# Saving the last states of seven scans on VectorE instead of ScalarE

## The reference

```
delta = softplus(dt @ wdt.T + bdt)
A = -exp(Alog)
dA = exp(delta[..., None] * A)                          # [rows, 1024 channels, 16 states]
dBu = (delta * u)[..., None] * Bm[:, :, None, :]
def step(h, t):
    h = dA_t * h + dBu_t
    return h, einsum('bdn,bn->bd', h, C_t)              # y of one row
```

## Time and profile before

| | |
|---|---|
| median of 3 runs | 7626.0 us (7614.66 to 7628.69) |
| the profiled execution | 7626.0 us, span 7624.1 us |
| TensorE | busy 6846.7 us, 90% |
| VectorE | busy 6908.3 us, 91% |
| ScalarE | busy 6185.3 us, 81% |
| GpSimd | busy 6963.5 us, 91% |
| mean granted TensorE clock | 0.972 |

### The profile page before, as it was taken

How to read it: one execution, slowest core, us unless ns; L and a number is a source line. 1 busy time by engine, 2 the same in 40 slices (tenths; PEclk the granted TensorE clock), 3 DMA queues, 4 the chain that set the end, 5 groups by cost and what they waited for, 6 DMA issues and landing times. The chain is left out here.

```text
span 7624.1 us, 137978 instructions
## 1 busy us (share of the span) xinstructions
PE 6846.7 (90%) x32682; PEld 4032.5 (53%) x32682; DVE 6908.3 (91%) x9409; ACT 6185.3 (81%) x12569; POOL 6963.5 (91%) x3774
## 2 busy tenths in 40 slices
PE   6899989999898989999898999999888999999889
PEld 3455555555555555555555555555555555555455
DVE  2799999999899999999899999999899999999766
ACT  1788888888888888888788888888888888888645
POOL 0899999999899999999999999999999999999678
PEclk8999999999999999999999999999999999999989
DMA  8444445444444553444445544444354444444555
GB/s 257 145 137 131 128 139 150 109 138 139 128 134 127 147 148 107 141 139 137 122 127 149 148 104 144 137 136 133 119 150 140 112 144 135 136 133 130 147 194 171
DMA packets 605613, 1066.05 MB, mean 140 GB/s; under 512 B 113584, under 2 KB 221872, under 8 KB 596336
## 3 DMA queue, kind: packets, MB, share of 16 engines
q1 hardware_dynamic: 602704, 1055.84, 46.9%
q10 hardware_dynamic: 2080, 1.05, 0.0%
HBM read 926.61 MB, written 130.05 MB: 139 GB/s over the span
## 5 line engine op out<-in xcount | busy, mean ns | idle before, releaser
L692 POOL TENSOR_TENSOR dBu<-Bb,du 128x1024 f32<-128x1024 f32 x2048 | 4786.0, 2364 | 80.0 <-DVE hV L1177 45.4
L1177 DVE TENSOR_TENSOR_SCAN scans<-scans,state,dBu 128x512 f32<-128x512 f32 x2304 | 2907.6, 1283 | 453.0 <-ACT scans L808 374.6
L808 ACT ACTIVATE scans<-delta,A 128x512 f32<-128x512 f32 x4096 | 2806.4, 697 | 506.4 <-DVE hR L1177 216.3
L1031 PE MATMUL yT<-ident,hC 128*128 128x128 f32 x9216 | 1399.6, 281 | 329.1 <-DVE hC L1193 317.4
L1193 DVE TENSOR_TENSOR hC<-scans,Cb 128x512 f32<-128x512 f32 x2304 | 1565.5, 681 | 18.0 <-PE yT L1031 17.9
L701 POOL TENSOR_TENSOR hR<-hR,Cb 128x512 f32<-128x512 f32 x1024 | 1293.3, 1275 | 213.5 <-ACT state L819 210.4
L1031 PEld LDWEIGHTS yT<-ident,hC 128*128 128x128 f32 x9216 | 1057.8, 143 | 758.7 <-DVE hC L1193 526.0
L1177 DVE TENSOR_TENSOR_SCAN hR<-scans,state,dBu 128x512 f32<-128x512 f32 x1024 | 1293.6, 1263 | 0.2
L1024 PE MATMUL bg<-u,comb 128*128 128x512 f32 x2112 | 989.4, 594 | 2.2 <-DMA comb<-comb_scratch 1.3
L1177 DVE TENSOR_TENSOR_SCAN hV<-scans,state,dBu 128x512 f32<-128x512 f32 x768 | 968.8, 1261 | 15.4 <-ACT scans L808 14.2
L963 PE MATMUL bg<-hT,win_u 128*128 128x512 f32 x2112 | 965.4, 598 | 0.9 <-ACT hT L728 0.9
(11 more groups left out here) (165 smaller groups left out, 7609.7 us busy)
## 6 DMA issues: line engine op xcount, KB each, us to landing
comb<-pre_scratch SPq DMA_DIRECT2D x1040, 256.0 KB, 4.6
Bb<-bc_scratch SPq DMA_DIRECT2D x264, 512.0 KB, 7.9
Cb<-bc_scratch SPq DMA_DIRECT2D x264, 512.0 KB, 8.7
win_u<-in_win SPq DMA_DIRECT2D x264, 256.0 KB, 4.9
pre_scratch<-pre SPq DMA_DIRECT2D x264, 256.0 KB, 3.8
comb<-comb_scratch SPq DMA_DIRECT2D x66, 1024.0 KB, 9.3
win_z<-in_win SPq DMA_DIRECT2D x257, 256.0 KB, 2.7
part_scratch<-pre SPq DMA_DIRECT2D x132, 256.0 KB, 2.0
```

The lines of the kernel that those rows point to most:

```text
L692: pool.tensor_tensor(dBu[:, q % AHEAD], Bb[:, 2 * q:2 * q + 2, :], du[:, j % 2, :].unsqueeze(1).broadcast_to([P, 2, T]), ALU.mult).then_in ...
L808: act.activation(dA[dA_bank(v, j, n)][:], delta[:, j % 2, :], ACT.Exp, scale=A[:, v % 2, j * N + n:j * N + n + 1]).then_inc(dA_made, 1)
L1031: ins = nc.tensor.matmul(yT[:, tt * P:(tt + 1) * P], product[:, tt * P:(tt + 1) * P], ident[:], start=first and tt == 0, stop=False, is_tr ...
L1177: nc.vector.tensor_tensor_scan(to, dA[dA_bank(v, j, n)][:], dBu[:, q % AHEAD, k, :], state[:, c:c + 1], ALU.mult, ALU.add).then_inc(h_made, 1)
```

## The change

The four copies of a tile leave ScalarE's queue and go into VectorE's, behind the other work of the pair in which the last state copied is scanned: states 3 and 4 behind pair 2, state 7 behind pair 3, states 1, 5 and 9 behind pair 4, state 11 behind pair 5. Each has a wait for its scan. SyncE's wait before it overwrites `C` names GpSimd's product (`hR_made`) instead of TensorE's use of that product (`hR_used`).

```diff
                         if 2 * q in ASIDE or 2 * q + 1 in ASIDE:
-                            sp.wait_ge(hR_used, aside(last, 2 * q + 2) + R0)
+                            sp.wait_ge(hR_made, aside(last, 2 * q + 2))
...
-            def keep_states(g, j, n):
-
-                for ns, places, saved in [(ns, hR, aside_saved) for ns in COPIES] + [(TURNED, hV, turned_saved)]:
-                    if n != ns[-1] + 3:
-                        continue
-                    act.wait_ge(h_made, g * N + ns[-1] + 1 + H0)
-                    k = (ASIDE if places is hR else TURNED).index(ns[0])
-                    step = ns[1] - ns[0] if len(ns) > 1 else 1
-                    act.copy(state[:, j * N + ns[0]:j * N + ns[-1] + 1:step],
-                             places[:, k:k + len(ns), T - 1]).then_inc(saved, 1)
...
                             step_dA(g, j, v, 2 * q)
-                            keep_states(g, j, 2 * q)
...
                             step_dA(g, j, v, 2 * q + 1)
-                            keep_states(g, j, 2 * q + 1)
...
+                            for n in pair:
+                                for ns, places, saved in [(ns, hR, aside_saved) for ns in COPIES] + [(TURNED, hV, turned_saved)]:
+                                    if n != ns[-1]:
+                                        continue
+                                    dve.wait_ge(h_made, g * N + n + 1 + H0)
+                                    k = (ASIDE if places is hR else TURNED).index(ns[0])
+                                    step = ns[1] - ns[0] if len(ns) > 1 else 1
+                                    nc.vector.tensor_copy(state[:, j * N + ns[0]:j * N + n + 1:step],
+                                                          places[:, k:k + len(ns), T - 1]).then_inc(saved, 1)
```

## The result

The changed kernel takes 7678.9 us (median of 4 runs, 7674.8 to 7684.3) against 7626.0 for the kernel before. It is slower, as forecast, but by 53 us where 161 were forecast. The ratio, 1.0075 with an interval of 1.0060 to 1.0089, counts three further runs of the changed kernel (7681.6 to 7685.6) and comes to 57 us. The profiled execution of the changed kernel has a span of 7682.2 us, 58 more than before.

What follows compares the result with a forecast made beforehand. VectorE's own order of work, with ScalarE's gaps in it, was taken to set the 27.2 us tile. Costs of 282 us, less 26, 64 and 31, gave +161 us on 7626.0: 7787 us, range 7632 to 8170.

Steps and rivals of the forecast that it cites:

- rival A: On VectorE, the one-element copies wait for GpSimd as well: +380 us more, 8170 us; chance 0.14.
- the two-element copy: VectorE's copy of states 3 and 4: waits 0.1 us a tile, bounds 0 and 2.36, as GpSimd's next product needs it.
- rival B: GpSimd gains no lead and both multi-element copies meet it by chance: 2.0 us instead of 0.8, 8090 us; chance 0.10.
- the seventh tile: One tile of eight, where ScalarE's table loads already hold VectorE 2.76 us: turned copy's cost not paid, 26 us back.
- VectorE's lateness: In the scan stage, a later VectorE waits less for ScalarE: 0.25 us per tile, 64 us off; bounds 0 and 1.0.
- C: In the scan stage, no copy this small waits for GpSimd: 7637 us; chance 0.13.
- D: Faster: ScalarE is the bound in more tiles, the full 0.36 us per tile leaves VectorE's waits: 7590 us; chance 0.08.
- ScalarE's relief: Four copies leaving ScalarE's queue shorten VectorE's waits by 0.12 us per tile, 31 us; bounds 0 and 92 us.
- I can't tell which and take the middle, 0.7, with 0.1 more: VectorE's copy of states 1, 5, 9: 0.7 us waiting for GpSimd, 0.1 for lost overlap; bounds 0 and 1.38.
- the meeting: VectorE's copy of 1, 5, 9 and GpSimd's `delta` arrive within 0.1 us: just before waits almost nothing, just behind 1.28 us.
- The four copies' place in the queue: Four copies on VectorE take 0.05 us each in its queue: 0.20 us per tile, 51 us.
- The range of the likeliest case: Copy of 1, 5, 9 against `delta`: won every time about +25 (7650 us), lost every time about +385 (8010 us).

Runs made afterwards that it cites:

- E1: The changed kernel with each copy of several states split into one-element copies, seven a tile, all on VectorE: 7634.7 us.
- E5: The changed kernel plus a two-element copy of hR into a spare tile ahead of each one-element copy (states 7 and 11): 8056.3 us.
- E4: The kernel before, ScalarE's copies kept, plus four VectorE copies of a spare SBUF tile at the change's places, nobody waiting for them: 7833.6 us.
- E8: The changed kernel with three one-element copies of a spare tile on VectorE directly ahead of the three-element copy: 7773.7 us.
- E3: E1 plus four ScalarE copies of a spare tile at its old places, which nobody waits for: 7636.9 us.

## Why the prediction was wrong, point by point

**Right.** That VectorE waits for the GpSimd instruction in flight and ends just behind it (E1, E5 and the tiles above; three copies of E4 waited for more than one); that two and three elements do and one doesn't, so rival A had no ground. A's price was 380 us more, and E5, which makes it come true, is 377 above the changed kernel. Right as well: that the two-element copy costs about 0.1 us a tile since GpSimd waits for it (0.06 measured; rival B is what E4 has, where that tie is missing); that the seventh tile pays nothing (in the changed kernel its copies don't wait at all, and E8 shows its stall taking up the waiting where they do); that VectorE's lateness is partly taken up by its waits for ScalarE; SyncE's wait at 0. C and D fell: the small copies do wait, and ScalarE's relief is 2 us.

**Wrong.** The step that failed is "I can't tell which and take the middle, 0.7, with 0.1 more". It gave 0.8 us in 224 tiles, 179 us. Measured: 86 us. For most tiles the meeting was placed rightly, within 0.1 us, and so were the prices on its sides (nearly 0, and up to 1.3 us). But one price for seven tiles of a chunk is what the runs contradict. In the fifth and sixth tile there is no meeting: all 64 copies come late and pay 0.67 us each, 43 us. In the first four 43 of 128 pay, 1.01 us each, 43 us, and in the eighth none. The 0.1 more isn't seen.

The two tiles could be told apart in the trace of the kernel before. There too the scan of state 9 in the fifth tile and that of state 8 in the sixth wait for ScalarE, 0.42 and 0.63 us on average, between the place of the copy of states 3 and 4 and that of the turned one:

```profile
3839.12 1.28 DVE L1177 TENSOR_TENSOR_SCAN hV<-scans,state,dBu 128x512 f32<-128x512 f32 x1 [0.43 <-ACT scans L808]
...
3864.39 1.29 DVE L1177 TENSOR_TENSOR_SCAN scans<-scans,state,dBu 128x512 f32<-128x512 f32 x1 [0.59 <-ACT scans L808]
```

For the other tiles a slip of 0.04 us hid the answer. 0.09 us before the end of the product (3813.14 + 0.68 = 3813.82) is 3813.73, not 3813.77. With two copies' 0.10 that is 3813.83, 0.02 ahead of `delta` at 3813.85, which is the side and about the distance that most tiles show. The working was hardly good to 0.02 us, but it would have leaned to the cheap side.

**Luck.** The middle, 0.7 of 1.28, stands for 122 lost meetings, and 107 copies waited. That these are close is chance: 64 of the 107 come from tiles that always lose, and what they pay is 0.80 us on average, not 1.28.

**Smaller sizes that were off.** The four copies' place in the queue was put at 51 us. The rows give 0.05 us for the copy of states 3 and 4 (3838.34 to 3838.39), but nothing for the one of state 7: from `hC` to the next scan it is 0.71 us with that copy between them (3840.80 to 3841.51) and 0.71 without a copy. At these places the next scan starts only behind the end of the product (0.68 us long) with or without a copy, and the copy fits into that gap. With 0.01 us each for the turned copy that didn't wait (0.72) and for that of state 11, it is about 0.07 us a tile, 18 us. The waits for ScalarE were to fall by 64 us for VectorE's lateness and 31 for the relief, 95 together; they fell by 52, of which E3 gives the relief 2.

**The range of the likeliest case** was not added up from its own terms. Won every time they give 77 - 64 - 31 = -18 us (7608), not +25; lost every time 77 + 224 x 1.38 - 95 = +291 (7917), and the +385 leaves out the 95.

**The sum with what was measured:** 18 + 16 + 86 = 120, less the 52 by which the waits for ScalarE fell: 68 us. The scan stage grew by 64, the span by 58, the medians by 53. So the forecast was 136 us too high in costs and 43 too high in what it took off, and the second hid a part of the first.

**What stays open.** In 38 of the 43 tiles among the first four that wait, the copy starts 0.03 us or more behind `delta`, in nearly all of them because the scan of state 8 or 9 started some 0.04 to 0.1 us late; what holds that scan isn't shown. In four others the copy starts up to 0.02 us ahead of `delta`, as in the tile at 1552, and still waits, while most copies that start so don't. The last of the 43, in the first tile of all, takes 0.21 us. Why these wait isn't settled.

## What to carry to other kernels

Before a small copy is moved between engines, ask what its form does beside GpSimd: here an SBUF-to-SBUF copy of two or three elements took up to 1.3 us (2.1 in E5), and the same data in copies of one element took 0.14 each. The price was the rest of GpSimd's instruction in flight, but for three copies of E4, so two queues that meet at the same point each tile make it nearly all or nothing: a shift of 0.18 us was worth some 100 us in this kernel. When a forecast comes down to such a meeting, the two ends are the forecast. Read the meeting in every kind of tile before one price is put on all: here two tiles in eight had a wait of their own just ahead of it, in the trace of the kernel before.

## What the runs showed of the hardware that I had not expected

The wait can be escaped by 0.02 us: a copy that started at 3844.54 beside a GpSimd instruction recorded from 3843.32 to 3844.60 and another from 3844.56 took its usual 0.16 us. With both at 1552.15 it took 1.30. And a dependence can hide the wait: a copy that GpSimd's next products wait for can't wait for those products (0.20 us against 1.04 in E4), only for the one before them. So the same copy is dearer when GpSimd doesn't need it. Third, a copy need not get in at the next end of a GpSimd instruction: three of the 237 that waited in E4 were passed over three times and took 5.2 to 6.5 us.
